# A buffer of their own for the rotary sums, rotary products a row block later, and another place for the first block sums in a one-core transformer layer

## The reference

```python
q = (xn @ wq).reshape(b, s, 16, 192)           # 128 plain + 64 rotary features a head
q_nope, q_pe = q[..., :128], q[..., 128:]
kva = xn @ wkv_a                               # 128 latent + 64 rotary features
ckv = rmsnorm(kva[..., :128]) * kv_norm_scale
k_nope, v = split(ckv @ wkv_b)
q_pe, k_pe = rope(q_pe), rope(kva[..., 128:])  # x1*cos - x2*sin, x2*cos + x1*sin
scores = concat(q_nope, q_pe) @ concat(k_nope, k_pe).T * 192 ** -0.5
out = softmax(causal(scores)) @ v @ wo
mixed = einsum('btd,rde->bte', x, factors) / sqrt(8) + bias
return x + out + mixed
```

## Time and profile before

| what | us |
|---|---|
| median of 3 runs (lowest, highest) | 1534.71 (1534.16, 1536.88) |
| the profiled execution, a run of its own | 1535.01 |
| its span, first to last instruction | 1533.2 |
| TensorE busy in that span | 1465.0 |
| VectorE, ScalarE, GpSimd busy | 1038.2, 1011.1, 1036.3 |
| granted TensorE clock over the span | 1.00 |

### The profile page before, as it was taken

One profiled execution on the slowest core, in us unless ns is written; L12 is line 12 of the kernel. 1 busy time (PEld: TensorE's weight loads), 2 busy tenths in 40 slices (PEclk: granted clock), 3 DMA queues, 4 the chain that ended last, 5 costly groups with the idle time before them and its releaser, 6 DMA issues.

```text
span 1533.2 us, 27332 instructions
## 1 busy us (share of the span) xinstructions
PE 1465.0 (96%) x8340; PEld 794.8 (52%) x8340; DVE 1038.2 (68%) x2627; ACT 1011.1 (66%) x2584; POOL 1036.3 (68%) x1081
## 2 busy tenths in 40 slices
PE   6899999999999999999999999999999999999987
PEld 5544555555554545555555555555555555555553
DVE  7877777777877766665566566656656666676676
ACT  7878777787876686666566666666546656554554
POOL 3688787776665796676577766667647766664563
PEclk9999999999999999999999999999999999999999
DMA  6599999888877788688677877767867668664554
GB/s 198 154 196 210 208 187 203 191 168 170 152 162 147 164 167 152 156 162 171 147 147 137 151 151 161 153 134 164 165 132 142 137 138 155 123 154 102 118 129 112
DMA packets 652256, 240.53 MB, mean 157 GB/s; under 512 B 599888, under 2 KB 614736, under 8 KB 651728
## 3 DMA queue, kind: packets, MB, share of 16 engines
q1 hardware_dynamic: 652112, 238.79, 74.6%
HBM read 75.10 MB, written 20.97 MB: 63 GB/s over the span
## 4 chain that ended last, share of the span: by engine, by line
PE 44%; DVE 7%; ACT 6%; issue 3%; POOL 2%; DMA 0%; DVEq 0%; ACTq 0%; POOLq 0%; SPq 0%
PE ps L570 9%; PE ps L572 9%; PE ps L571 9%; PE ps L766 3%; PE ps L772 3%; PE ps L767 3%; PE ps L771 3%; PE ps L768 3%; ACT ex L1052 3%; DVE ps L1467 2%; DVE acc L1518 1%; ACT st L1062 1%; POOL q L1776 1%; DVE gm L1465 1%; POOL st L1792 1%
## 5 line engine op out<-in xcount | busy, mean ns | idle before, releaser
L1792 POOL TENSOR_TENSOR st<-ex,st 128x512 f16<-128x512 f32 (+3 forms) x640 | 638.1, 1017 | 417.9 <-ACT st L1062 409.5
L1052 ACT ACTIVATE ex<-ps,nm,scales 128x512 f32<-128x512 f32 (+3 forms) x640 | 452.7, 711 | 448.5 <-DVE nm L1484 448.0
L1465 DVE TENSOR_REDUCE gm<-ps 128x1 f32<-128x512 f32 (+1 forms) x384 | 250.6, 671 | 183.5 <-PE ps L772 178.7
L1062 ACT ACTIVATE st<-ex 128x512 f16<-128x512 f32 (+3 forms) x640 | 342.9, 563 | 5.9
L1518 DVE SCALAR_TENSOR_TENSOR acc<-ps,rden,acc 128x512 f32<-128x512 f32 x256 | 189.6, 745 | 68.1 <-PE ps L572 67.9
L766 PE MATMUL ps<-kTh,q 128*128 128x512 f16 (+3 forms) x640 | 222.2, 347 | 13.5 <-POOL q L1754 5.5
L570 PE MATMUL ps<-pT,vH 128*128 128x512 f16 (+3 forms) x640 | 222.1, 347 | 2.1 <-DMA pT<-st 2.1
L772 PE MATMUL ps<-kRl,q 128*128 128x512 f16 (+3 forms) x640 | 222.1, 347 | 0.0
L771 PE MATMUL ps<-kRh,q 128*128 128x512 f16 (+3 forms) x640 | 222.1, 347 | 0.0
L571 PE MATMUL ps<-pT,vH 128*128 128x512 f16 (+3 forms) x640 | 222.1, 347 | 0.0
L768 PE MATMUL ps<-kTh,q 128*128 128x512 f16 (+3 forms) x640 | 222.1, 347 | 0.0
(11 more groups left out here) (313 smaller groups left out, 2478.2 us busy)
## 6 DMA issues: line engine op xcount, KB each, us to landing
wS<-w_abs SPq DMA_DIRECT2D x48, 256.0 KB, 3.0
wV<-w_vo SPq DMA_DIRECT2D x48, 256.0 KB, 2.9
pT<-st SPq DMA_TRANSPOSE x640, 3.3
wS<-w_abs SPq DMA_DIRECT2D x24, 384.0 KB, 3.5
fland<-factors_in SPq DMA_DIRECT2D x28, 256.0 KB, 3.1
wP<-w_pe SPq DMA_DIRECT2D x24, 256.0 KB, 3.8
wsq<-wq_in SPq DMA_DIRECT2D x16, 256.0 KB, 3.8
wso<-wo_in SPq DMA_DIRECT2D x16, 256.0 KB, 3.0
```

Of the source, the lines that this page charges most:

```text
L1052: e.activation(ex[:, n % NEX, 0:keys], s_bank(n)[:, 0:keys], ACT.Exp, bias=nm[:, (i * QT + r) % 4:(i * QT + r) % 4 + 1], scale=scales[:, p ...
L1062: e.activation(stage(n, keys)[:, :, 0, :], ex[:, n % NEX, 0:keys].rearrange("p (t n) -> p t n", n=P), ACT.Copy).then_inc(z["a_pH"], 1)
L1465: e.tensor_reduce(m, b, AX_X, ALU.max).then_inc(z["v_max"], 1)
L1792: e.tensor_tensor(s[:, :, 1, :], ex[:, n % NEX, 0:keys].rearrange("p (t n) -> p t n", n=P), s[:, :, 0, :], ALU.subtract).then_inc(z["g_pL" ...
```

## The change

It has these parts.

1. Head pair 0's block sums leave units 0 and 1 and are done in unit 9, between those of pairs 4 and 5 (`SUMMED`, `sum_slots`). The semaphore counts follow the new order. The transposes of (1, 3) no longer wait for them.
2. The 32-bit weights of heads 0, 1 and 2 are made by GpSimd from `wA` (two additions of 128x256 a head, "wf" fills in (0,0), (0,2) and (1,0), after the low parts of the row block) into parts of `wS`, of `wa` and of `ktmp`; ScalarE's copies from PSUM for these heads (L999) are gone. VectorE's next writes of `wA` wait for GpSimd's reading.
3. GpSimd's rotary sum goes to a buffer of its own (`turned_q`, in `wa`) for every pair but the first, as a fill "turn". VectorE's products wait for the sum before (`g_rot`), no longer for the low parts; the sum waits for those. From unit 16 on the products stand in row block 3 in place of 2.
4. ScalarE's copies c11, c22 and c21 go ahead of the row block's exponentials, GpSimd's ahead of its low parts.
5. `SOON` has m2 first, so that VectorE adds m2 before the other work due with it in unit 15; the banks 5 to 7 are given out anew.

```diff
+SUMMED = (1, 2, 3, 4, 0, 5, 6, 7)
+
+
+def sums_before(m):
+
+    return SUMMED.index(m)
+
+
+def sum_slots(m):
+
+    if m == 0:
+        i = 2 * SUMMED[SUMMED.index(0) + 1] - 1
+        return (i, 0), [(i, 1), (i, 1), (i, 2), (i, 2)], [(i, 2), (i, 2), (i, 3), (i, 3)], (i, 3)
+    i = 2 * m
+    if m == H // 2 - 1:
+        return (i - 1, 3), [(i, 0)] * 4, [(i, 1)] * 4, (i, 1)
+    return (i - 1, 3), [(i, 0), (i, 0), (i, 2), (i, 3)], [(i, 1), (i, 1), (i, 3), (i + 1, 0)], (i + 1, 0)
...
         if (i, r) == pe_at(e) and (e < H or e % H == 0):
-            out += [("pe", e), ("rot", e)]
-        if e > H and e % H and (i, r) == (e - 2, 2):
-            out.append(("rot", e))
+            out += [("pe", e), ("rot", e), ("turn", e)]
+        if e > H and e % H and (i, r) == (e - 2, 3):
+            out += [("rot", e), ("turn", e)]
...
         out += [("sum_hi", (m, n)) for n in range(4) if high[n] == (i, r)]
         out += [("sum_lo", (m, n)) for n in range(4) if low[n] == (i, r)]
+    if (i, r) in KEPT:
+        out.append(("wf", KEPT.index((i, r))))
     for k in range(1, NC):
         if (i, r) in token_slots(k):
             out.append(("tok", (k, token_slots(k).index((i, r)))))
@@ -275,12 +284,13 @@
 
 
 IN_BANKS = ("q", "pe", "tkv", "wvo", "tq", "wabs", "out", "ffn", "m1", "m2", "m7")
...
-SOON = {"nv": 0, "nf": 1, "out": 2, "tq": 3, "q": 4, "nrm": 5}
+SOON = {"m2": -1, "nv": 0, "nf": 1, "out": 2, "tq": 3, "q": 4, "nrm": 5}
 
 
...
-        first_f = pT[:, 1, 2 * NT - 2:2 * NT, :].rearrange("p t n -> p (t n)").bitcast(F32)
+        kept = wS[:, :, :].rearrange("p b n -> p (b n)").bitcast(F32)
+        latent_w = wa[:, :, :, :].rearrange("p a k n -> p (a k n)").bitcast(F32)
+        turned_q = latent_w[:, 0:CH]
...
 
-        def weights_f(m, h):
-
-            return ((wf, first_f) if m == 0 else (kf, wf))[h][:, 0:E]
+        def weights_f(m, h, n):
+
+            if m == 0:
+                return (kept[:, n * HC:(n + 1) * HC] if h == 0 else (kept[:, 12 * P:14 * P], latent_w[:, CH:CH + HC])[n])
+            return (kf, wf)[h][:, n * HC:(n + 1) * HC]
+
+        def rotary(i):
+
+            return rot[:, 0, :] if i < 2 else turned_q
 
         def two(ap):
...
-                        e.wait_ge(z["a_wf"], count(user))
+                    if user[0] == "wabs" and user[1] >= len(KEPT):
+                        e.wait_ge(z["a_wf"], user[1] - len(KEPT) + 1)
                 return bank(key)
 
...
-            def weights_sums(h):
+            def weights_kept(h):
 
                 m = h // 2
                 e.wait_ge(z["v_wabs"], h + 1)
-                if h == 1:
-                    e.wait_ge(z["d_xTs"], 16 * (NC - 1))
-                elif h == 2:
-                    e.wait_ge(z["g_kk"], NP)
-                elif h >= 3:
-
-                    e.wait_ge(z["g_sum"], 6 * m if h % 2 else 6 * m - 2)
-                e.activation(weights_f(m, h % 2), bank(("wabs", h)), ACT.Copy, scale=1.0 / WS).then_inc(z["a_wf"], 1)
+                if m >= 2:
+
+                    e.wait_ge(z["g_sum"], 6 * sums_before(m - 1) + (6 if h % 2 else 4))
...
-                e.activation(q[:, i % 2, 2, :], rot[:, 0, :], ACT.Copy).then_inc(z["a_parts"], 1)
+                e.activation(q[:, i % 2, 2, :], rotary(i), ACT.Copy).then_inc(z["a_parts"], 1)
 
             def exps(i, r, p):
...
                         if soon and kind == "pv" and n[0] < NU - 2:
                             fill(kind, n)
-                    early = ("q", "wo", "sqv", "m6", "c11", "c22") + (("sq1",) if i == 0 else ())
-
+                    early = ("q", "wo", "sqv", "m6") + (("sq1",) if i == 0 else ())
+
+                    ahead = ("m1", "c11", "c22", "c21")
                     late = ("parts",) if last >= 2 and (r < 2 or i == 0) else ()
                     for kind, n in fills(i, r):
-                        if kind == "m1":
+                        if kind in ahead:
                             fill(kind, n)
                     for p in range(last + 1):
                         exps(i, r, p)
@@ -1193,7 +1208,7 @@
                     for kind, n in fills(i, r):
                         if soon and kind == "pv" and n[0] < NU - 2:
                             continue
-                        if kind != "m1" and (last < 2 or (r >= 2 and i) or kind not in early + late):
+                        if kind not in ahead and (last < 2 or (r >= 2 and i) or kind not in early + late):
                             fill(kind, n)
 
...
                     e.wait_ge(z[f"d_sA{h % 2}"], 16 * (h // 2))
+                if 2 <= h < 2 + len(KEPT):
+                    e.wait_ge(z["g_wf"], h - 1)
...
                 e.wait_ge(z["p_pe"], i // 2 + 1)
-                if i:
+                if i == 2:
                     e.wait_ge(z["g_parts"], 2 * i)
+                elif i:
...
+            def weights_kept(h):
+
+                e.wait_ge(z["v_wabs"], h + 1)
+                if h == 1:
+                    e.wait_ge(z["p_kva"], NT)
+                if h == 2:
+                    e.wait_ge(z["g_kk"], NP)
+                for n in range(2):
+                    at = slice(n * HC, (n + 1) * HC)
+                    ins = e.tensor_tensor(weights_f(h // 2, h % 2, n), wA[:, h % 2, 0, at], wA[:, h % 2, 1, at], ALU.add)
+                ins.then_inc(z["g_wf"], 1)
...
                 e.wait_ge(z["v_pe"], i // 2 + 1)
-                e.tensor_tensor(rot[:, 0, :], rot[:, 0, :], rot[:, 1, :], ALU.add).then_inc(z["g_rot"], 1)
+                if i:
+                    e.wait_ge(z["g_parts"], 2 * i)
+                    e.wait_ge(z["p_kva"], NT)
+                e.tensor_tensor(rotary(i), rot[:, 0, :], rot[:, 1, :], ALU.add).then_inc(z["g_rot"], 1)
...
                 for r in range(QT):
+                    for kind, n in fills(i, r):
+                        if kind in ("c11", "c22", "c21"):
+                            block_low(kind, n)
                     if i < NU:
                         for p in range(chunk(i) + 1):
...
                         e.wait_ge(z["p_pv"], i - 1)
-                if (i, r, p) == (1, 3, 0):
-
-                    e.wait_ge(z["g_sum"], 6)
```

More of the change, by code:

```diff
@@ L264, in fills @@
             out.append(("bias", k * QT + r))
-    for m in range(G0):
-        if r == 3 and i == sum_slot(m):
+    for m in SUMMED:
+        at, high, low, _ = sum_slots(m)
+        if at == (i, r):
             out.append(("sum", m))
-        high, low, _ = sum_parts(m)
         out += [("sum_hi", (m, n)) for n in range(4) if high[n] == (i, r)]
         out += [("sum_lo", (m, n)) for n in range(4) if low[n] == (i, r)]
+    if (i, r) in KEPT:
+        out.append(("wf", KEPT.index((i, r))))
     for k in range(1, NC):
@@ L1775, in rope_parts @@
                     dst = slice((2 * half + 1 - i % 2) * HALF, (2 * half + 2 - i % 2) * HALF)
[L1776 removed]
+                    e.tensor_tensor(hi[dst, :], rotary(i)[src, :], hi[src, :], ALU.subtract).then_inc(
                         z["g_parts"], 1)
@@ L1843, in _ @@
                             token_step(*n)
-                        elif kind in ("c11", "c22", "c21"):
-                            block_low(kind, n)
-                        elif kind == "rot":
+                        elif kind == "wf":
+                            weights_kept(n)
+                        elif kind == "turn":
                             q_rope(n)
@@ L2071, in _ @@
                             load_vo(i - 1)
-                    for m in range(G0):
-                        if (i, r) == sum_parts(m)[2]:
+                    for m in SUMMED:
+                        if (i, r) == sum_slots(m)[3]:
                             store_sums(m)
```

72 lines of the change are left out of this document (37 added, 35 removed).

## The result

The changed kernel takes 1511.92 us in the median of 4 runs (1509.5 to 1513.49), the kernel before beside it 1535.8 (1534.16 to 1537.23). The ratio is 0.9843, with a 95% interval of 0.9826 to 0.9861: 24 us less. The profiled execution took 1509.5 us, with a span of 1507.6.

A forecast was written before the change was run, and what follows sets the result against it. TensorE, busy 1465.0 of 1533.2 us, was taken as the bound. Terms -12.8 - 6.0 - 0.2 - 0.8 - 1.4 - 1.8 + 1.0 = -22.0 against 1535.0 gave 1513.0 us; 8-in-10 range 1505.5 to 1524.

The forecast's parts named there:

- chunk 1: Units 32 to 47: all 12.1 us of m6 gaps go, plus 0.7 outside the odd units: -12.8, bounds -10 and -13.6.
- chunk 0, units 48 to 61: Rotary part and copies take most of 6.7 us of snapshot waits in odd units: -6.0, bounds -3 and -9.
- unit 62 and start of unit 63: One low part fewer ahead of TensorE's 3.28 us wait for c21 at unit 63's start: -0.8, bounds 0 and -1.6.
- chunk 2: Idle time there is 2.2 us; -0.2 taken, between 0 and that.
- unit 15: With m2 first, TensorE's 1.44 us wait for VectorE's m2 sum goes: -1.4, bounds 0 and -1.5.
- units 0 to 2: Waits ahead of (1, 1) and (2, 0) shrink as sums and copies leave: -1.8, bounds 0 and -3.6.
- unit 9: Pair 0's sums, added where TensorE is never idle, cost TensorE time: +1.0, bounds +0.5 and +2.9.
- The chain from VectorE's wait on L1776 to the m6 gap: Unit 35: VectorE's 3.17 us wait on low parts delays offset, exponentials and snapshot, leaving TensorE 2.01 us idle ahead of m6.
- the signs that were named: Profile signs, including chunk 1's odd-unit m6 gaps under 0.2 us and those six units' idle time near 1 us.
- What is late next: Chunk 1: products now precede the maxima of (35, 0), which were expected no later than now.
- that is mostly not won: Chunk 0: the 0.40 us ahead of unit 55's first score mostly stays; 0.1 a unit counted, 0.6 in all.
- The loads as the next bound: Chunk 0: m1's weights land 3.0 us after issue, about where m1 starts now, so they become the next bound.

The follow-up runs named there:

- p_buffer: The kernel before with only GpSimd's rotary sum in its own buffer, VectorE's products staying in row block 2: 1523.08 us against 1537.9.
- p_late: The kernel before with only the rotary products moved to row block 3, the sum still in place in `rot`: 1518.44 us.
- a_mixed: The changed kernel with rotary products and their sum back in row block 2 for chunks 2 and 1: 1507.62 us against 1534.58.
- a_loads: The changed kernel with the loads of m1's, m2's and m6's weights issued one row block earlier: 1511.5 us.
- p_copies: The kernel before with only copies c11, c22, c21 moved ahead of exponentials and low parts: 1525.84 us against 1537.9.

## Why the prediction was right, step by step

The forecast was 1513.0 and the time is 1511.92; the forecast change of 22.0 us stands against 23.9 between the medians, and 25.6 between the two profiled spans. The terms, each by the windows of the profile:

| step | forecast | between the two profiles |
|---|---|---|
| chunk 1 | -12.8 | -12.1 |
| chunk 0, units 48 to 61 | -6.0 | -7.4 |
| unit 62 and start of unit 63 | -0.8 | -0.9 |
| chunk 2 | -0.2 | +0.6 |
| unit 15 | -1.4 | -1.6 |
| units 0 to 2 | -1.8 | -2.8 (some -2.0 over all runs) |
| unit 9 | +1.0 | +1.0 |
| ahead of unit 0, and unit 63 | 0 | -1.7, -0.7 |

**What held.** The chain from VectorE's wait on L1776 to the m6 gap was the cause in chunk 1: the buffer alone took the gaps away (p_buffer). The m2 step came out as worked out; so did the claim that nothing slows in chunk 2 through the copies, and unit 62. Of the signs that were named, one failed: the idle time of the six odd units of chunk 1 is 3.8 us, not near 1.

**Chunk 1, right in size for a partly wrong reason.** "What is late next" was answered with the maxima of (35, 0), "no later than now". They are not later: they start 1.87 us into unit 35, against 1.91 before. But TensorE arrives 2 us sooner, and the copy to `oT` behind those maxima is late by 0.62 us in six units. I looked one instruction too short down VectorE's queue. What came in made up for it. The m6 waits were worth 2.14 to 2.16 each from start to start, 12.9 and not 12.1. The waits ahead of m3, which I left in, went with the copies, some 1.5. And 0.27 us in each even unit and 0.3 in unit 33, from the copies too, make 2.3 where 0.7 was forecast. Against that stand 4.7 us for the copy, 0.78 in each odd unit. I had also counted products and wait as parts of one gain. By p_buffer and p_late each alone takes out the m6 gaps, and the new place costs those 4.7 us in chunk 1 (a_mixed) that the kernel did not have to pay. So the size came out by errors that cancel.

**Chunk 0, under-sized.** The step "that is mostly not won" on the first-score waits is the one that failed: the even units shortened by 0.57 each (0.41 in unit 50), 3.3 us in all, where I had 0.6. In exchange the odd units won 3.8, where nearly all of the -6.0 was forecast, as their weights came late (0.31 to 1.55 us a unit). The sum of that step was rounded from 6.2 to 6.0 as well. The loads as the next bound were right for the kernel as it is, but worth only 1.5 us (a_loads), since the copy to `oT` stands right behind.

**Chunk 2, wrong in sign.** I had -0.2 and it is +0.6, 0.11 in each of six odd units. p_late has it and p_buffer and p_copies have not, so it is the products' place, through the copy to `oT` as the rows of unit 19 show.

**Units 0 to 2, right in size by luck.** The -1.8 was to come from the waits at (1, 1) and (2, 0) in unit 1. On average over the runs with and without these parts, unit 1 gives 0.3 us, well within its own scatter of 1.7, and unit 2 takes 0.3 back. The 2.0 us come from the wait of 1.80 in unit 0 at 73.57, behind ScalarE's copy of head 1, which stands in no term of the sum: the forecast looked at what the three copies held up in unit 1 and not in unit 0. The -2.8 between the two profiles has another 0.8 us in it, since unit 1 of the changed kernel's profile (32.71) is the shortest of the seven.

**The price of the sums.** +1.0 was taken between 0.84 and 2.6, a middle value that no row of before singled out; both sums took 0.60 + 0.42. That the rule would make it 2.6 depended on GpSimd being inside a low part twice, and it was there once, at its end.

**The rest.** The time ahead of unit 0 lies between 53.25 and 54.74 in the changed kernel and its variants, and unit 63 between 22.78 and 25.23 over all runs, in no order that goes with the edits. So a microsecond or two of a single time come from there. The profiled execution after has the shortest first stretch of all, 53.25, and nearly the shortest last, 22.80; these 2.4 us may well be why the spans differ by 25.6 and the medians by 23.9. What sets the two stretches was not looked into.

## What to carry to other kernels

A gap on the busiest engine can come from a buffer four queue steps away: follow it back until an engine waits for a reader, and give that one a buffer before moving any work. When a stall is taken out, list everything in that engine's queue up to the next thing the busiest engine needs, not only the next instruction; here the copy two places on became the next wait twice. With stages cut at the same instruction in each profile, edits worth 0.1 us a unit can be told apart in single runs, where whole times of one kernel scatter by 4 (1509.5 to 1513.49). And a forecast term that matches in size should still be looked up in its own unit: that of units 0 to 2 matched through another wait.
